# Statistics pieces summed in another order and partly ahead of the LoRA passage, and a weight chunk clipped ahead of a low half

## The chip, the cores and the metric

The kernel runs on one core of a Trainium2 chip. The metric is the device time of one execution in microseconds, median of the runs. TensorE is called PE, VectorE DVE, ScalarE ACT, GpSimd POOL; SP is the sync engine, which here only issues DMAs ("SPq" in rows; "ACTq" is ACT's own issuing).

## The reference

The input is 32 sequences of 64 tokens of width 1024, 2048 tokens in all. Cut to what matters:

```
y   = einsum('bct,bcd->bdt', x, W_cond[cond_id])          # 64x64 per sequence
h   = relu(layernorm(y @ gw1.T + gb1)); gates = h @ gw2.T + gb2; top-2 of 8, softmax, capacity
x1  = x + y @ weight.T + lora(y, gates)                   # LoRA of rank 16 for each of 8 experts
z   = x1 @ W1[adapter_id[b]].T                            # one of 8 full 1024x1024 matrices per sequence
# bitlinear(x, w): s = mean|w|; q = round(clip(w/(s+eps), -1, 1)); x @ (q*s).T
out = x1 + bitlinear(bitlinear(z, w_gate) * bitlinear(z, w_up), w_down)       # inner width 2752
```

So the mean of |w| over each of w_gate, w_up and w_down (2.8 million values each) must be known before the first weight of that layer is quantized.

## The kernel before

Every engine has a hand-written program; their order against each other comes from semaphores alone. The text splits each float32 operand into a float16 high part (ACT) and a low part (DVE). The stages:

**Main loop** (to about 245 us). `main(t)` multiplies token tile t (128 tokens, 16 tiles) by the first weight. Around it run the gate network (`quarter_mean`, `quarter_prod`, `quarter_top` on DVE), `w_step` (splits the adapter matrices and stores them to `w1s_scratch`), and `sum_gate(p)`, ACT's 16 sums of |w_gate|, placed by the table `SUMS_AT`; SP's `load_sum` fetches them.

**Passage** (about 235 to 261 us). PE transposes the weighted LoRA activations, ACT and DVE split them (`tmpw_high`, `tmpw_low`), PE does `lora(0)`.

**Slots k = 0 to 12** (261 to 450 us), and then some more. A slot is a pair of sequences with the same adapter; `linear(k)` multiplies it by its matrix (48 matmuls, L845), `linear_t(k-1)` transposes the slot before (8 matmuls, L678). An adapter in use is a rank; `load_rank(r)` (L519, two DMA transposes of 2 MB) fills one of two buffers of `w1_t`, and is on SP's queue. Into the same slots are laid `turn_x1`, `lora` and `x1_sum` of token tiles (tables `TURNS`, `LORAS`), and 24 statistics pieces of 0.92 MB: even p are w_up and are summed by ACT (`sum_up`, L1153), odd p are w_down and are summed by DVE (`sum_down`, L1586). `PIECES_AT` says in which slot k a piece is summed. ACT and DVE do the sums of slot k first, then `x1_part`/`low_x1`, `copy_z`, `x1_sum`, `high_z`/`low_z`. The pieces lie in six buffers; a load waits for the sum that frees its buffer, on the queue that issues it. `high_z` and `low_z` read two registers by TENSOR_LOAD (L391).

**Token group 0** (about 475 to 713 us). The 22 chunks n of 128 inner rows are loaded, clipped (`quantize`, DVE L1617), rounded (`round_q`, ACT L1184; the gate rows of even chunks DVE), transposed (`turn_q`, PE L884), taken out of PSUM (`store_q`, ACT L1200), summed into seven combinations (`turn_a`, `turn_b` on DVE) and stored by SP for the later groups; `gate_up(n)` (PE L900, 32 matmuls) multiplies them by the 512 tokens of the group, `scale_gate` (ACT L1205) and `product` (DVE L1661) join them, `high_inter` (ACT) and `low_inter` (DVE L1634, 128x1792) split the result. A `store_q` of an even chunk's w_down waits for the store of `wb` of the pair before. The kinds are 0 gate, 1 up, 2 down; `turn_q(2,...)` of kind 2 shares its PSUM bank with kind 0 of chunks below 3.

**Groups 1 to 3** (780 to 1398 us) use the stored combinations (L965, L1002).

Of the kernel before, what the change touches and what calls it, by code (L numbers as in the profile page):

```python
# [110 lines left out]
def build_program(nc, x, adapter_id, cond_id, cond_w, w0, lora_a, lora_b, gw1, gb1, ln_g, ln_b, gw2, gb2,  # L111
                  w1, w_gate, w_up, w_down, out):
    ctx = ExitStack()
    with ctx:
# [148 lines left out]
        index_step = sem("index_step")  # L263
# [17 lines left out]
        gate_step = sem("gate_step")  # L281
        quarter_step = sem("quarter_step")
        var_ready = sem("var_ready")
        gap_ready = sem("gap_ready")
# [3 lines left out]
        gate_exp = sem("gate_exp")  # L288
# [12 lines left out]
        w1_loaded = sem("w1_loaded")  # L301
        piece_loaded = [sem(f"piece_loaded{i}") for i in range(NSD)]
# [111 lines left out]

        def load_piece(eng, p):
            at_p, n = piece_cols(p)
            if p >= NSD:
                eng.wait_ge((up_summed, down_summed)[p % 2], (p - NSD) // 2 + 1)
            eng.dma_start(stat_in[p % NSD][:, 0:n], (up_flat, down_flat)[p % 2][:, at_p:at_p + n])\
               .then_inc(piece_loaded[p % NSD], 16)  # L420

        def piece_count(p):

            return 16 * (gate_pieces(p % NSD) + p // NSD + 1)
# [22 lines left out]

        def gate_pieces(s):

            return len(range(s, NPIECE_G, NSG)) if s < NSG else 0  # L450
# [9 lines left out]
        def _(sp):  # L460
# [16 lines left out]
            def load_sum(p):  # L477
                s = p % NSG
                if p < NSG:
                    sp.wait_ge(ag_high, 3)  # L480
                    sp.wait_ge(ag_low, 3)
                wait_if(sp, gate_summed, p - NSG + 1)
                sp.dma_start(stat_gate[s], gate_flat[:, p * PIECE_G:(p + 1) * PIECE_G]).then_inc(piece_loaded[s], 16)
# [190 lines left out]
        def _(pe):  # L674
# [333 lines left out]

            turn_q(2, 0, 1, (2,))
            gate_up(1, 1)  # L1010
# [21 lines left out]
        def _(act):  # L1032
# [34 lines left out]
            def sum_gate(p):  # L1067
                s = p % NSG
                act.wait_ge(piece_loaded[s], 16 * (p // NSG + 1))
                act.activation(stat_gate[s], stat_gate[s], ACT.Abs, accum_out=stat_g[:, p:p + 1]).then_inc(gate_summed, 1)  # L1070
# [25 lines left out]
            for m in range(1, NT + 1):  # L1096
# [9 lines left out]
                if m == NT - 3:  # L1106
                    gate_root(3)
                    act.wait_ge(gap_ready, 1)
                    act.activation(row[:, 5, :], row[:, 4, :], ACT.Exp).then_inc(gate_exp, 1)
# [8 lines left out]
                for p in SUMS_AT.get(m, ()):  # L1118
                    sum_gate(p)
            for i in range(2):  # L1120
                act.wait_ge(tmpw_transposed, i + 1)
                high(tmpw_t[:, 0, i * D:(i + 1) * D], pair[i][:, :], 1.0).then_inc(tmpw_high, 1)
# [27 lines left out]
            def sum_up(p):  # L1150
                at_p, n = piece_cols(p)
                act.wait_ge(piece_loaded[p % NSD], piece_count(p))
                act.activation(stat_in[p % NSD][:, 0:n], stat_in[p % NSD][:, 0:n], ACT.Abs,  # L1153
                               accum_out=stat_u[:, p // 2:p // 2 + 1]).then_inc(up_summed, 1)

            for k in range(LAST_TURN + 1):
# [97 lines left out]
            scale_gate(0, 0)  # L1254
            high_z(k - 1)
# [46 lines left out]
        def _(v):  # L1302
# [9 lines left out]
            def then(instruction):  # L1312
                step[0] += 1
                instruction.then_inc(index_step, 1)
                v.wait_ge(index_step, step[0])
# [25 lines left out]
            v.tensor_scalar(ix_lt, nums, ix_part, None, ALU.is_gt).then_inc(index_step, 1)  # L1341
            v.tensor_scalar(ix_le, nums, ix_part, None, ALU.is_ge).then_inc(index_step, 1)
            v.tensor_scalar(ix_shift, nums, 1.0, ix_part, ALU.add, ALU.is_equal).then_inc(index_step, 1)
# [63 lines left out]
            count = [0]  # L1407

            def gthen(instruction):
                count[0] += 1  # L1410
                instruction.then_inc(gate_step, 1)
                v.wait_ge(gate_step, count[0])
# [66 lines left out]
            def gate_weights():  # L1479
                v.tensor_tensor(gap, p2, p1, ALU.subtract).then_inc(gap_ready, 1)  # L1480
# [3 lines left out]
                v.wait_ge(gate_exp, 1)  # L1484
# [71 lines left out]
            with v.If(used > NADP - 1):  # L1556
                w_step(NT - 2)
                w_step(NT - 1)
            for i in range(2):
# [22 lines left out]

            def sum_down(p):
                at_p, n = piece_cols(p)
                v.wait_ge(piece_loaded[p % NSD], piece_count(p))
                v.tensor_reduce(stat_d[:, p // 2:p // 2 + 1], stat_in[p % NSD][:, 0:n], X, ALU.add,  # L1586
                                apply_absolute_value=True).then_inc(down_summed, 1)
# [209 lines left out]
            turn_a(1, 1)  # L1797
            product(0, 0, 0, 0)
# [7 lines left out]
            for m in range(1, 4):  # L1806
                if m > 1:
                    product(m - 1, (m - 1) % 2, (m - 1) // 2, (m - 1) // 2 % 2)
                if m == 3:
                    low_inter(0, 0)  # L1810
                quantize(m + 2, m % 2, m // 2 + 1)
# [13 lines left out]
            for m in range(16, IC + 1):  # L1825
                product(m - 1, (m - 1) % 2, (m - 1) // 2, (m - 1) // 2 % 2)
                if m % 2 == 1:
                    low_inter((m - 3) // 2, (m - 3) // 2 % 2)
                if m < IC - 2:
                    quantize(m + 2, m % 2, m // 2 + 1, last=(m == IC - 3))  # L1830
# [38 lines left out]
```

## Time and profile before

| what | value |
|---|---|
| median of 3 runs | 1390.0 us (1388.51 to 1393.92) |
| the profiled execution's own time | 1399.73 us |
| its span | 1398.1 us |
| granted TensorE clock, mean | 0.987 |
| busy: PE / DVE / ACT / POOL | 1334.7 / 727.5 / 410.5 / 141.8 us |
| mean DMA rate | 216 GB/s |

The span is the time from the first to the last instruction of the profiled execution. PE is busy for 95% of it, so the time can only fall where PE stands still, runs at the lower clock or has less to do.

### The profile page before, as it was taken

What the parts mean: (1) busy time and instruction counts of PE and PEld (TensorE: products, weight loads), DVE (VectorE), ACT (ScalarE), POOL (GpSimd) and SP (SyncE); (2) the same over time, 40 slices, a digit from 0 to 9 for tenths busy, and PEclk for the clock granted to TensorE, in tenths of its full rate; (3) what the DMA queues carried; (4) which work ended last, traced back from release to release, by engine and by line L of the source; (5) the groups of instructions that cost most, each with busy time, mean ns of one, the idle gap of its engine ahead of it and who ended that gap; (6) DMA issues with size and microseconds to landing.
All of it is one profiled execution on the core that took longest, in us unless ns stands there. A gap on an engine that the chain in (4) does not pass through costs nothing.

```text
span 1398.1 us, 23462 instructions
## 1 busy us (share of the span) xinstructions
PE 1334.7 (95%) x8864; PEld 848.3 (61%) x8864; DVE 727.5 (52%) x1187; ACT 410.5 (29%) x456; POOL 141.8 (10%) x79
## 2 busy tenths in 40 slices
PE   6999999999799998999999999999999999999998
PEld 5566664444345544555444788844888844888833
DVE  5447656443344336888855355572455581455521
ACT  3445432232231426777730011110111110111100
POOL 3200000000000000000000132210133310232200
PEclk9999999999899999999999999999999999999999
DMA  9899983999948347999774644444633355544344
GB/s 250 285 388 352 342 307 82 308 287 242 257 170 201 87 141 249 332 333 331 251 267 162 219 158 158 147 184 161 222 139 144 141 215 180 186 158 158 136 184 143
DMA packets 171950, 302.48 MB, mean 216 GB/s; under 512 B 99009, under 2 KB 131009, under 8 KB 164065
## 3 DMA queue, kind: packets, MB, share of 16 engines
q1 hardware_dynamic: 158496, 260.00, 57.0%
q10 hardware_dynamic: 12352, 40.90, 8.1%
q8 instruction: 52, 0.85, 0.2%
q0 software_dynamic: 1024, 0.53, 0.2%
q14 instruction: 26, 0.20, 0.0%
HBM read 212.39 MB, written 68.03 MB: 201 GB/s over the span
## 4 chain that ended last, share of the span: by engine, by line
PE 71%; DMA 7%; DVE 7%; issue 5%; ACT 4%; SPq 3%; ACTq 1%; POOL 1%; POOLq 0%; DVEq 0%
PE pair L965 26%; PE pair L1002 14%; PE pair L763 11%; PE pair L845 10%; SPq L519 3%; DMA wb_scratch<-region_q 2%; DMA region_q<-wb_scratch 2%; PE pair L731 2%; PE pair L900 2%; PE pair L678 2%; ACT region_q L1184 2%; PE pair L746 2%; DVE region_q L1617 1%; DMA region_w<-in_L_ffn_w_down 1%; PE pair L781 1%
## 5 line engine op out<-in xcount | busy, mean ns | idle before, releaser
L965 PE MATMUL pair<-act_t,region_q 128*128 128x256 f16 x3696 | 404.0, 273 | 0.6 <-DMA region_q<-wa_scratch 0.6
L965 PEld LDWEIGHTS pair<-act_t,region_q 128*128 128x128 f16 x3696 | 361.6, 98 | 43.3 <-DMA region_q<-wa_scratch 1.1
L1002 PE MATMUL pair<-region_q,region_w 128*128 128x512 f16 x1232 | 269.3, 381 | 6.6 <-DMA region_q<-wb_scratch 6.3
L663 POOL TENSOR_TENSOR region_w<-region_q,region_w 128x1792 f32 (+1 forms) x33 | 118.4, 3587 | 1157.7 <-ACT region_w L1209 1157.7
L1002 PEld LDWEIGHTS pair<-region_q,region_w 128*128 128x128 f16 x1232 | 120.4, 98 | 154.2 <-DMA region_q<-wb_scratch 8.1
L845 PE MATMUL pair<-region_w,act_t 128*128 x816 | 186.7, 386 | 3.7 <-issue 2.1
L763 PE MATMUL pair<-region_w,act_t 128*128 128x512 f16 x768 | 169.5, 380 | 0.0
L900 PE MATMUL pair<-act_t,region_q 128*128 128x512 f16 x704 | 157.6, 383 | 0.0
L845 PEld LDWEIGHTS pair<-region_w,act_t 128*128 x816 | 81.0, 99 | 98.1 <-issue 11.6
L1215 ACT ACTIVATE region_q<-pair 128x512 f32<-128x512 f32 x33 | 19.7, 598 | 403.3 <-PE pair L965 403.3
L1306 DVE SCALAR_TENSOR_TENSOR act_t<-pair,act_t 128x512 f32 (+1 forms) x66 | 61.1, 947 | 146.2 <-ACT act_t L1034 146.2
L763 PEld LDWEIGHTS pair<-region_w,act_t 128*128 128x128 f16 x768 | 75.1, 98 | 87.6 <-issue 1.3
L900 PEld LDWEIGHTS pair<-act_t,region_q 128*128 128x128 f16 x704 | 68.6, 99 | 79.8 <-issue 3.0
L1034 ACT ACTIVATE act_t<-pair 128x512 f32 (+1 forms) x66 | 51.3, 804 | 155.5 <-PE pair L731 54.7
L1209 ACT ACTIVATE region_w<-region_q 128x1792 f32 (+1 forms) x44 | 74.6, 1695 | 65.2 <-DVE region_q L1654 65.2
L1728 DVE SCALAR_TENSOR_TENSOR region_q<-pair,out_c,region_q 128x512 f32<-128x512 f32 x32 | 24.0, 750 | 112.1 <-PE pair L1002 112.0
L1200 ACT ACTIVATE region_q<-pair 128x1024 f16<-128x1024 int16 x66 | 63.2, 1034 | 27.1 <-DMA wb_scratch<-region_q 26.1
L1681 DVE TENSOR_TENSOR region_q<-pair,region_q 128x512 f32<-128x512 f32 x33 | 22.8, 692 | 90.1 <-PE pair L965 90.1
L678 PE MATMUL pair<-ident,region_q 128*128 128x128 f32 x328 | 48.0, 297 | 20.1 <-DVE act_t L1306 17.0
L1184 ACT ACTIVATE region_q<-region_q,inv 128x1024 f32<-128x1024 f32 x55 | 59.8, 1150 | 19.9 <-DVE region_q L1617 19.9
L1674 DVE TENSOR_TENSOR region_q<-pair,region_q 128x512 f32<-128x512 f32 x33 | 22.8, 692 | 75.6 <-PE pair L965 75.6
L678 PEld LDWEIGHTS pair<-ident,region_q 128*128 128x128 f32 x328 | 41.5, 153 | 29.1 <-issue 14.5
(187 smaller groups left out, 1024.9 us busy)
## 6 DMA issues: line engine op xcount, KB each, us to landing
region_q<-wa_scratch SPq DMA_DIRECT2D x33, 1792.0 KB, 7.4
region_q<-wb_scratch SPq DMA_DIRECT2D x28, 1408.0 KB, 6.1
region_q<-in_L_cond_weight SPq DMA_DIRECT2D x40, 512.0 KB, 8.6
w1s_scratch<-region_q ACTq DMA_DIRECT2D x40, 512.0 KB, 6.1
wa_scratch<-region_q SPq DMA_DIRECT2D x22, 896.0 KB, 5.9
region_w<-in_L_ffn_w_gate SPq DMA_DIRECT2D x16, 688.0 KB, 9.2
wb_scratch<-region_q SPq DMA_DIRECT2D x11, 896.0 KB, 4.1
region_q<-in_L_ffn_w_gate SPq DMA_DIRECT2D x19, 512.0 KB, 5.2
```

Source lines behind the costliest of these rows:

```text
L663: pool.tensor_tensor(at(iop[:, 1], u), st[s][:, 0:7], at(iop[:, 0], u), ALU.subtract)\
L678: mm = pe.transpose(dst[:, k * P:(k + 1) * P], src[:, k * P:(k + 1) * P], idn[:, :])
L763: mm = pe.matmul(acc[:, h * H:(h + 1) * H], act_t[:, a, k, t * P:(t + 1) * P], w0_t[:, 4 * h:4 * h + 4, b, k, :], start=(k == 0 and a + b ...
L845: mm = pe.matmul(pair[s][:, h * H:(h + 1) * H], act_t[:, a, c, ds(at, P)], w1_t[:, ds(buf, 1), b, c, h * H:(h + 1) * H].rearrange("p x o - ...
L900: mm = pe.matmul(dst, wa[s][:, first + k // 4, (k % 4) * P:(k % 4 + 1) * P], act_t[:, a, k, 0:GRP], start=(k == 0 and a == 0), stop=(k == ...
L965: mm = pe.matmul(bank(s_bank, b)[:, (1 - h) * HALF:(2 - h) * HALF], ring_a[s][:, h, o_a, k], moving[a], start=(opens and h == 1 and k == 0 ...
L1002: mm = pe.matmul(bank(s_bank, b), iop[:, a, p, o_a, tp * P:(tp + 1) * P], ring_b[r][:, p], start=(opens and p == 0 and a == 0), stop=(not ...
L1034: return act.activation(dst, src, ACT.Copy, scale=scale)
L1184: act.activation(tile, tile, ACT.Copy, bias=ROUND, scale=inv[:, kind:kind + 1])\
L1200: act.activation(dst, src, ACT.Copy, bias=-BITS).then_inc(q_out[kind], 1)
L1209: act.activation(at(iop[:, 0], u), st[s][:, 0:7], ACT.Copy).then_inc(inter_high, 1)
L1306: return v.scalar_tensor_tensor(out=dst, in0=src, scalar=scale, in1=hi, op0=ALU.mult, op1=ALU.subtract)
```

## The change

The semaphores `index_step` and `gate_step` become one, `gap_ready` joins `var_ready` and `gate_exp` joins `gate_std`; w_gate's sums get semaphores of their own (`gate_loaded`). The last six sums of |w_gate| move up. Pieces 0 to 3 are loaded ahead of `load_rank(0)` and summed ahead of the passage's splits; the slots' table of pieces changes; at the start of group 0 `gate_up(1)` comes ahead of the down rows of chunk 2, and chunk 3 is clipped earlier; in the loop of group 0 `quantize` comes ahead of `low_inter`.

```
-SUMS_AT = {**{m: (m - 1,) for m in range(1, 11)}, 11: (10, 11), 12: (12, 13), 13: (14, 15)}
+SUMS_AT = {**{m: (m - 1,) for m in range(1, 11)}, 11: (10, 11, 12), 12: (13, 14, 15)}
-PIECES_AT = {0: range(0, 4), 1: range(4, 6), 2: range(6, 8), 3: range(8, 12), 5: range(12, 18), 9: range(18, 24)}
-LATE_PIECES_AT = 6
+PIECES_AT = {0: range(4, 8), 1: range(8, 10), 3: range(10, 16), 6: range(16, 22), 9: range(22, 24)}
...
+        def piece_slot(p):
+            return p if p < 4 else (p - 4) % NSD
         def load_piece(eng, p):
...
-            if p >= NSD:
-                eng.wait_ge((up_summed, down_summed)[p % 2], (p - NSD) // 2 + 1)
+            if 4 <= p < 8 or p >= 10:
+                eng.wait_ge((up_summed, down_summed)[p % 2], (p - (4 if p < 8 else NSD)) // 2 + 1)
...
 # SP
-            sp.wait_ge(y_done, NT)
-            sp.wait_ge(quarter_step, 3 * (QT + 1))
-            sp.wait_ge(gate_summed, NPIECE_G)
             for s in range(4):
                 sp.wait_ge(w_stored[s], stores(0))
-            load_rank(0)
...
             for p in range(4):
                 load_piece(sp, p)
+            sp.wait_ge(y_done, NT)
+            sp.wait_ge(quarter_step, 3 * (QT + 1))
+            sp.wait_ge(gate_summed, NPIECE_G)
+            load_rank(0)
+            for p in range(4, 8):
+                load_piece(sp, p)
             sp.wait_ge(tmpw_transposed, 2)
-            for p in range(4, 6):
+            for p in range(8, 10):
                 load_piece(sp, p)
...
                 if r == 1:
-                    for p in range(6, 12):
+                    for p in range(10, 16):
                         load_piece(sp, p)
                 if r == 2:
-                    for p in range(12, 18):
+                    for p in range(16, 22):
                         load_piece(sp, p)
 # PE
-            turn_q(2, 0, 1, (2,))
             gate_up(1, 1)
+            turn_q(2, 0, 1, (2,))
 # ACT
+            for p in (0, 2):
+                sum_up(p)
             for i in range(2):
                 act.wait_ge(tmpw_transposed, i + 1)
...
-                if k == LATE_PIECES_AT:
-                    for p in range(18, NPIECE):
+                if k == 6:
+                    for p in range(22, NPIECE):
                         load_piece(act, p)
...
             scale_gate(0, 0)
+            store_q(2, 0, 1, (0, 1))
             high_z(k - 1)
...
-                store_q(m + 1, (m + 1) % 2, (m + 1) // 2, (0, 1, 2) if m == 1 else (2, 0, 1))
+                if m == 2:
+                    store_q(2, 0, 1, (2,))
+                if m > 1:
+                    store_q(m + 1, (m + 1) % 2, (m + 1) // 2)
 # DVE
+            for p in (1, 3):
+                sum_down(p)
             for i in range(2):
                 v.wait_ge(tmpw_high, i + 1)
...
             turn_a(1, 1)
+            quantize(3, 1, 1)
             product(0, 0, 0, 0)
...
                     product(m - 1, (c - 1) % 2, 2 * i + (c - 1) // 2, (c - 1) // 2 % 2)
+                    quantize(m + 2, c % 2, 2 * i + c // 2 + 1)
                     if c % 2 == 1:
                         low_inter(2 * i + (c - 3) // 2, (c - 3) // 2 % 2)
-                    quantize(m + 2, c % 2, 2 * i + c // 2 + 1)
```

The same swap of `quantize` and `low_inter` stands in the rounds ahead of and behind the loop.

On SP's queue, between the end of the main loop's loads and the wait for `main_done` that precedes `load_rank(1)`, before (the piece loads are L419, the rank's transposes L519, and rank 0's two stand ahead of these rows):

```order
L419 DMA region_q<-in_L_ffn_w_up 128x1835
L419 DMA region_q<-in_L_ffn_w_down 128x1835
L419 DMA region_q<-in_L_ffn_w_up 128x1835
L419 DMA region_q<-in_L_ffn_w_down 128x1835
L419 DMA region_w<-in_L_ffn_w_up 128x1835 [waits tmpw_transposed]
L419 DMA region_w<-in_L_ffn_w_down 128x1835
L541 COMPARE_AND_BRANCH [waits main_done]
L519 DMA_TRANSPOSE region_w<-w1s_scratch 128x8x1024 [waits w1_loaded]
L519 DMA_TRANSPOSE region_w<-w1s_scratch 128x8x1024
```

And the same place of the changed kernel, up to the same point (L421 and L516 are its lines for these):

```order
L421 DMA region_q<-in_L_ffn_w_up 128x1835
L421 DMA region_q<-in_L_ffn_w_down 128x1835
L421 DMA region_q<-in_L_ffn_w_up 128x1835
L421 DMA region_q<-in_L_ffn_w_down 128x1835
L516 DMA_TRANSPOSE region_w<-w1s_scratch 128x8x1024 [waits gate_summed,quarter_step,y_done]
L516 DMA_TRANSPOSE region_w<-w1s_scratch 128x8x1024
L421 DMA region_q<-in_L_ffn_w_up 128x1835 [waits up_summed]
L421 DMA region_q<-in_L_ffn_w_down 128x1835 [waits down_summed]
L421 DMA region_q<-in_L_ffn_w_up 128x1835 [waits up_summed]
L421 DMA region_q<-in_L_ffn_w_down 128x1835 [waits down_summed]
L421 DMA region_w<-in_L_ffn_w_up 128x1835 [waits tmpw_transposed]
L421 DMA region_w<-in_L_ffn_w_down 128x1835
```

Four pieces have moved ahead of rank 0's transposes, and four more, which wait for the sums of the first four, stand between rank 0's and rank 1's.

On PE, behind the last transposition of a slot and up to the loop of group 0, before (L884 is `turn_q`, L900 `gate_up`):

```order
L928 UNCONDITIONAL_BRANCH
L884 MATMUL pair<-ident,region_q 128x128 [waits q_out0,rounded2]
L884 MATMUL pair<-ident,region_q 128x128 x7
L900 MATMUL pair<-act_t,region_q 128x512 [waits gate_scaled,q_out1,q_out0]
L900 MATMUL pair<-act_t,region_q 128x512 x31
L1012 UNCONDITIONAL_BRANCH [waits slots_done]
```

After:

```order
L927 UNCONDITIONAL_BRANCH
L899 MATMUL pair<-act_t,region_q 128x512 [waits gate_scaled,q_out1,q_out0]
L899 MATMUL pair<-act_t,region_q 128x512 x31
L883 MATMUL pair<-ident,region_q 128x128 [waits q_out0,rounded2]
L883 MATMUL pair<-ident,region_q 128x128 x7
L1011 UNCONDITIONAL_BRANCH [waits slots_done]
```

The 32 matmuls of `gate_up(1)` no longer stand behind the transposes that wait for ACT's `store_q` of chunk 2.

On DVE, in the body of the loop of group 0, from the product of an even chunk on, before:

```order
L1661 TENSOR_TENSOR region_q<-pair,region_q 128x2x256 [waits inter_low,gate_scaled]
L1634 ISA [waits inter_high]
L1634 TENSOR_TENSOR region_w<-region_q,region_w 128x1792
L1617 TENSOR_SCALAR region_q<-region_q,clip,nclip 128x1024 [waits wq_loaded1]
L1617 TENSOR_SCALAR region_q<-region_q,clip,nclip 128x1024 [waits wq_loaded3]
L1617 TENSOR_SCALAR region_q<-region_q,clip,nclip 128x1024 [waits wq_loaded5]
L1640 TENSOR_TENSOR region_q<-region_q 128x512 [waits q_out1,q_out0]
```

After:

```order
L1667 TENSOR_TENSOR region_q<-pair,region_q 128x2x256 [waits inter_low,gate_scaled]
L1623 TENSOR_SCALAR region_q<-region_q,clip,nclip 128x1024 [waits wq_loaded1]
L1623 TENSOR_SCALAR region_q<-region_q,clip,nclip 128x1024 [waits wq_loaded3]
L1623 TENSOR_SCALAR region_q<-region_q,clip,nclip 128x1024 [waits wq_loaded5]
L1640 ISA [waits inter_high]
L1640 TENSOR_TENSOR region_w<-region_q,region_w 128x1792
L1646 TENSOR_TENSOR region_q<-region_q 128x512 [waits q_out1,q_out0]
```

The low half (L1634, then L1640) now stands behind the three clips of the odd chunk, and still ahead of `turn_a`.

## Rows read from the trace of the kernel before

**Rows 1.** The page's chain that ended last, by engine

```profile
PE 71%; DMA 7%; DVE 7%; issue 5%; ACT 4%; SPq 3%; ACTq 1%; POOL 1%; POOLq 0%; DVEq 0%
```

**Rows 2.** PE's waits from 225 to 720 us: total us, times, longest

```profile
PE pair L678 <- DVE act_t L1306: 17.0, 5, 11.7
PE pair L884 <- ACT region_q L1184: 9.4, 18, 2.0
PE pair L884 <- ACT region_q L1200: 5.5, 2, 5.1
```

**Rows 3.** The chain in order of time around slot k = 5: start, us, what

```profile
341.53 14.86 DMA region_w<-in_L_ffn_w_down
...
359.86 1.94 PE pair L678 x8
361.80 7.05 PE pair L845 x24
...
369.72 5.18 PE pair L845 x24
```

**Rows 4.** One stretch by windows: busy us by engine, PEclk, DMA share, GB/s

```profile
353.00:358.00 5.00, 0.00 (x0) 0.00 (x0) 2.52 (x2) 3.22 (x4) 0.00 (x0) 0.50 1.14 321
```

**Rows 5.** SP's queue over time: the transposes of ranks 0, 1 and 2

```profile
235.45 16.09 SPq L519 DMA_TRANSPOSE region_w<-w1s_scratch  x2
...
257.36 30.76 SPq L519 DMA_TRANSPOSE region_w<-w1s_scratch  x2
...
299.01 39.95 SPq L519 DMA_TRANSPOSE region_w<-w1s_scratch  x2
```

**Rows 6.** The timeline between slots 2 and 3: idle before and its releaser in brackets

```profile
298.59 2.06 DVE L1586 TENSOR_REDUCE stat_d<-region_q 128x1 f32<-128x1835 f32 x1 [5.99 <-DMA region_q<-in_L_ffn_w_down]
...
302.04 1.07 PE L678 MATMUL pair<-ident,region_q 128*128 128x128 f32 x8 [1.81 <-DVE act_t L1306]
...
303.86 7.01 PE L845 MATMUL pair<-region_w,act_t 128*128 x24 [0.76 <-issue]
```

**Rows 7.** The timeline in slot 8, PE

```profile
398.22 1.09 PE L678 MATMUL pair<-ident,region_q 128*128 128x128 f32 x8 [2.38 <-DVE act_t L1306]
...
399.15 5.74 PE L845 MATMUL pair<-region_w,act_t 128*128 x18
```

**Rows 8.** Register loads on ACT from 389 to 397 us: ns min/median/max

```profile
L391 ACTq TENSOR_LOAD <-ixi x2: 1072/1130/1187, 392.7 to 394.1; - x2
```

**Rows 9.** Groups of the piece sums (of both, 4 more in region_w)

```profile
L1586 DVE TENSOR_REDUCE stat_d<-region_q 128x1 f32<-128x1835 f32 x8 | 16.4, 2060 | 18.9 <-DMA region_q<-in_L_ffn_w_down 18.9
...
L1153 ACT ACTIVATE region_q<-region_q 128x1835 f32<-128x1835 f32 x8 | 13.9, 1736 | 17.3 <-DMA region_q<-in_L_ffn_w_up 14.5 <-DVE region_q L1510 2.8
```

**Rows 10.** The timeline before and in the passage, ACT and DVE

```profile
215.35 0.14 DVE L1477 COPY region_w<-region_w 1x1 f32<-1x1 f32 x1
...
244.75 1.94 ACT L1034 ACTIVATE region_q<-pair 128x1024 f16<-128x1024 f32 x2 [9.44 <-PE pair L814]
...
254.69 1.22 DVE L1510 SCALAR_TENSOR_TENSOR region_q<-pair,act_t 128x1024 f32<-128x1024 f32 x1 [6.53 <-PE pair L781]
```

**Rows 11.** The timeline at the start of group 0, PE

```profile
514.13 7.07 PE L900 MATMUL pair<-act_t,region_q 128*128 128x512 f16 x32
...
527.20 1.01 PE L884 MATMUL pair<-ident,region_q 128*128 128x128 f16 x8 [5.12 <-ACT region_q L1200]
...
528.00 9.32 PE L900 MATMUL pair<-act_t,region_q 128*128 128x512 f16 x32
```

**Rows 12.** One pair of chunks in the loop of group 0, DVE and ACT

```profile
600.24 2.02 DVE L1634 TENSOR_TENSOR region_w<-region_q,region_w 128x1792 f32 x1
...
602.44 2.86 ACT L1200 ACTIVATE region_q<-pair 128x1024 f16<-128x1024 int16 x3 [2.89 <-DMA wb_scratch<-region_q]
```

**Rows 13.** The last chunk of group 0, ACT's rounding

```profile
694.96 1.15 ACT L1184 ACTIVATE region_q<-region_q,inv 128x1024 f32<-128x1024 f32 x1 [1.13 <-DVE region_q L1617]
...
696.35 2.19 ACT L1184 ACTIVATE region_q<-region_q,inv 128x1024 f32<-128x1024 f32 x2 [0.24 <-DVE region_q L1617]
```

More of the change, by code:

```diff
@@ L262, in build_program @@
         consts_ready = sem("consts_ready")
-        index_step = sem("index_step")
+        scalar_step = sem("scalar_step")
         index_sorted = sem("index_sorted")
@@ L301, in build_program @@
         w1_loaded = sem("w1_loaded")
+        gate_loaded = [sem(f"gate_loaded{i}") for i in range(NSG)]
         piece_loaded = [sem(f"piece_loaded{i}") for i in range(NSD)]
@@ L413, in piece_cols @@
             return p // 2 * PIECE, min(PIECE, INNER * D // P - p // 2 * PIECE)
+        def piece_slot(p):
+            return p if p < 4 else (p - 4) % NSD
         def load_piece(eng, p):
             at_p, n = piece_cols(p)
-            if p >= NSD:
-                eng.wait_ge((up_summed, down_summed)[p % 2], (p - NSD) // 2 + 1)
-            eng.dma_start(stat_in[p % NSD][:, 0:n], (up_flat, down_flat)[p % 2][:, at_p:at_p + n])\
-               .then_inc(piece_loaded[p % NSD], 16)
+            s = piece_slot(p)
+            if 4 <= p < 8 or p >= 10:
+                eng.wait_ge((up_summed, down_summed)[p % 2], (p - (4 if p < 8 else NSD)) // 2 + 1)
+            eng.dma_start(stat_in[s][:, 0:n], (up_flat, down_flat)[p % 2][:, at_p:at_p + n]).then_inc(piece_loaded[s], 16)
         def piece_count(p):
-            return 16 * (gate_pieces(p % NSD) + p // NSD + 1)
+            s = piece_slot(p)
+            return 16 * len([o for o in range(p + 1) if piece_slot(o) == s])
         def store_wa(eng, p, h, n):
@@ L446, in stores @@
             return 32 * (r + 1)
-        def gate_pieces(s):
-            return len(range(s, NPIECE_G, NSG)) if s < NSG else 0
         def x1_stores(i):
@@ L1007, in down @@
                                 mm.then_inc(dn_done if tp == 0 else step_done, 1)
+            gate_up(1, 1)
             turn_q(2, 0, 1, (2,))
-            gate_up(1, 1)
             pe.wait_ge(slots_done, 1)
@@ L1068, in sum_gate @@
                 s = p % NSG
-                act.wait_ge(piece_loaded[s], 16 * (p // NSG + 1))
+                act.wait_ge(gate_loaded[s], 16 * (p // NSG + 1))
                 act.activation(stat_gate[s], stat_gate[s], ACT.Abs, accum_out=stat_g[:, p:p + 1]).then_inc(gate_summed, 1)
@@ L1107, in _ @@
                     gate_root(3)
-                    act.wait_ge(gap_ready, 1)
-                    act.activation(row[:, 5, :], row[:, 4, :], ACT.Exp).then_inc(gate_exp, 1)
+                    act.wait_ge(var_ready, 5)
+                    act.activation(row[:, 5, :], row[:, 4, :], ACT.Exp).then_inc(gate_std, 1)
                 j = m - 1
@@ L1119, in _, with sum_up @@
                     sum_gate(p)
+            def sum_up(p):
+                at_p, n = piece_cols(p)
+                act.wait_ge(piece_loaded[piece_slot(p)], piece_count(p))
+                act.activation(stat_in[piece_slot(p)][:, 0:n], stat_in[piece_slot(p)][:, 0:n], ACT.Abs,
+                               accum_out=stat_u[:, p // 2:p // 2 + 1]).then_inc(up_summed, 1)
+            for p in (0, 2):
+                sum_up(p)
             for i in range(2):
@@ L1147, in high_z @@
                 high(act_t[:, 0, :, ds(d1, SEQ)], ps8[2][:, :, SEQ:P], ACT_SCALE).then_inc(z_high, 1)
[L1150 to L1154, printed above, removed]
             for k in range(LAST_TURN + 1):
@@ L1313, in then @@
                 step[0] += 1
-                instruction.then_inc(index_step, 1)
-                v.wait_ge(index_step, step[0])
+                instruction.then_inc(scalar_step, 1)
+                v.wait_ge(scalar_step, step[0])
             def compare(dst, row, column, op, scale=None):
@@ L1404, in main_part @@
                                        in1=rows_of(x_nat[slot]), op0=ALU.mult, op1=ALU.add).then_inc(acc_released, 1)
-            count = [0]
             def gthen(instruction):
-                count[0] += 1
-                instruction.then_inc(gate_step, 1)
-                v.wait_ge(gate_step, count[0])
+                step[0] += 1
+                instruction.then_inc(scalar_step, 1)
+                v.wait_ge(scalar_step, step[0])
             def per_channel(a, n=NT):
@@ L1558, in _, with sum_down @@
                 w_step(NT - 1)
+            def sum_down(p):
+                at_p, n = piece_cols(p)
+                v.wait_ge(piece_loaded[piece_slot(p)], piece_count(p))
+                v.tensor_reduce(stat_d[:, p // 2:p // 2 + 1], stat_in[piece_slot(p)][:, 0:n], X, ALU.add,
+                                apply_absolute_value=True).then_inc(down_summed, 1)
+            for p in (1, 3):
+                sum_down(p)
             for i in range(2):
@@ L1808, in _ @@
                     product(m - 1, (m - 1) % 2, (m - 1) // 2, (m - 1) // 2 % 2)
+                if m > 1:
+                    quantize(m + 2, m % 2, m // 2 + 1)
                 if m == 3:
                     low_inter(0, 0)
-                quantize(m + 2, m % 2, m // 2 + 1)
                 if m % 2 == 0:
@@ L1826, in _ @@
                 product(m - 1, (m - 1) % 2, (m - 1) // 2, (m - 1) // 2 % 2)
+                if m < IC - 2:
+                    quantize(m + 2, m % 2, m // 2 + 1, last=(m == IC - 3))
                 if m % 2 == 1:
                     low_inter((m - 3) // 2, (m - 3) // 2 % 2)
-                if m < IC - 2:
-                    quantize(m + 2, m % 2, m // 2 + 1, last=(m == IC - 3))
                 if m < IC and m % 2 == 0:
```

20 lines of the change are left out of this document (6 added, 14 removed).

## The prediction, as put on record before the changed kernel ran

> **What bounds the kernel now.** First the page's chain by engine: PE holds 71% of it, every other engine 7% or less [rows 1]. PE is busy for 95% of the span, so the time falls only where PE stands or runs at the lower clock; DVE and ACT have slack nearly everywhere, and the groups behind 780 us read nothing that the change touches. Then PE's waits from 225 to 720 us: 17.0 us in five waits of the slots' transposition (L678) for DVE's `copy_z` (L1306), one of them 11.7; 5.5 in two waits of `turn_q` (L884) for ACT's `store_q`, one of them 5.1; 9.4 in 18 waits of `turn_q` for ACT's rounding, none above 2.0 [rows 2]. The first two are places that the change touches. The chain around slot 5 shows what is late in the worst one: a transfer of a w_down piece of 14.86 us ends it at 341.53 + 14.86 = 356.4, and PE starts its transposition only at 359.86 [rows 3]. In the window 353 to 358 PE does nothing at all, DVE and ACT do sums, and the granted clock is 0.50 [rows 4], the lower level of 1.2 GHz; the first 24 matmuls behind it take 7.05 us, the next 24 take 5.18 [rows 3].
>
> Why so late: on SP's queue pieces 12 to 17 stand behind rank 2's transposes, which start at 299.01 and take 39.95 us [rows 5], so they are issued from 339.0 and are summed in slot 5, ahead of `copy_z`.
>
> **The stall of slot 5.** The change sums these pieces (p = 16 to 21 in its numbers) in slot 6 and issues them behind a rank 2 that has less beside it. What it removes: 11.7 of waiting [rows 2], 1.94 - 1.07 = 0.9 of slow transposition [rows 3, 6], 7.05 - 5.18 = 1.9 of slow matmuls [rows 3]: **14.5 us**, if the pieces are there in time.
>
> Are they? The two transposes of a rank move the same bytes each time and took 16.09 us for rank 0, 30.76 for rank 1, 39.95 for rank 2 [rows 5]. Rank 0 ran with no piece issued ahead of it, rank 1 and 2 with pieces of the same queue still in flight. In the change four pieces go ahead of rank 0; rank 0 itself waits for the last step of `quarter_top(2)`, whose last copy is at 215.35 [rows 10], so it starts at about 215.5, 20 us earlier than now. Pieces 4 to 9 follow at 231 to 251 as the sums in the passage free their buffers. Rank 1 still waits for `main_done` (257.36 [rows 5]); I take 16 to 22 us for it, since only the tail of pieces 8 and 9 is beside it, so it ends near 274 to 280 instead of 288. Pieces 10 to 15 are then issued some 10 us earlier than 6 to 11 are now, and land at about 291 (six pieces of 0.92 MB at the 321 GB/s of [rows 4] are 17 us). Rank 2 waits for slot 2 (299.01) as before, finds them landed, and ends at about 317; pieces 16 to 21 land by about 335, and slot 6 wants them at about 347. That is 12 us of slack; with a rank 2 as slow as the present 39.95, they would land near 356 and be 9 us late.
>
> Here a page of the Trainium skill speaks against such a reordering: "DMA: Bandwidth & Descriptors", section "Issuing engines are not separate DMA queues", says that transfers of all issuing engines interleave on the same 16 DMA engines, so order alone buys no bandwidth. The trace agrees in so far as the same transposes differ by 16.09 against 39.95 with pieces beside them. By that rule the wait only moves, which is the first rival below; the order still decides who is late.
>
> **Slots 2 and 3.** Between them PE waits 1.81 for `copy_z`, another 0.76 in front of the matmuls, and then runs 24 matmuls in 7.01 instead of 5.18, because DVE idled 5.99 us for a piece [rows 6]: 1.81 + 0.76 + 1.83 = 4.4. In the change slot 3 holds three sums on DVE instead of two (2.06 each, so 6.2 us [rows 9]), all landed 7 us ahead of it. Such a chain of three sums ahead of `copy_z` can leave a wait of its own; I put 0.3 to it. **4.1 us.**
>
> **Slot 8.** PE waits 2.38 and then does 18 matmuls in 5.74 [rows 7] where 18/24 of 5.18 are 3.9. In the same slot ACT's register loads take 1.1 us each [rows 8]; pieces 18 to 23 are in flight there (issued from ACT's queue in slot 6), and in the change only 22 and 23 are. The other waits of this kind without a cause share 17.0 - 11.7 - 2.38 - 1.81 = 1.1 us, so some 0.6 of 2.38 may stay: 1.8 + 1.8, say **3.5 us** (bounds 0 and 4.2).
>
> **The passage.** The new sums stand ahead of the splits. ACT's two take 2 x 1.74 = 3.5 us [rows 9], and it has 9.44 us of idle time ahead of its splits (L1034 [rows 10]): hidden. DVE's two take 4.1; they stand behind its last work of the main loop and push `tmpw_low` by about 3.5 us, and DVE's idle of 6.53 in front of L1510 [rows 10] takes that up: PE's `lora(0)` (L781), which waits for the low half, would still find it there with 1.7 us to spare. **0**; if that cover is gone, each us is one us of PE, and SP's pieces 8 and 9 behind it are late by as much. The upper bound is 4.1 lost. The sums of |w_gate| that move up lie in ACT's idle time of the main loop and only free rank 0 earlier.
>
> **Start of group 0.** Now the transposition of chunk 2's down rows waits 5.12 us for ACT, takes 1.01, and `gate_up(1)` follows in 9.32 where a run of the same 32 at full clock takes 7.07 [rows 11]: 5.12 + 1.01 + 9.32 = 15.4 from the end of `linear_t` at 522.1. In the change `gate_up(1)` goes first: 7.07, then 8 transpositions (0.6 at full clock) and a wait of about 1.2 before chunk 3's, since ACT must do `scale_gate` and `store_q` of kind 2 first: 8.9. That frees PE by 6.5 and starts `scale_gate` of chunk 1, and with it DVE, 8 us earlier. PE and the DVE-ACT chain drive the loop behind it together; I take **7.0**. The clips of chunk 3 (2 x 1 to 3 us) fit into DVE's wait for that product. Bounds: 4.0 (only the clock and a part of the wait) to 8.1.
>
> **The swap in the loop.** `low_inter` (2.02 us) now comes behind the clips of the odd chunk, which come 2 us earlier. ACT ahead of the odd chunk's `store_q` waits 2.89 us for the store of `wb` to land [rows 12], not for a clip, and PE's waits for rounding are half a us each [rows 2]. The even chunk's chain (clips, transposes, `turn_b`, store, `store_q`, rounding, `scale_gate`, product) doesn't contain the odd clips. **0** (bounds -3 to +3 over 9 pairs). Only in the last chunk, where there is no further pair, does ACT wait for clips, 1.13 and 0.24 [rows 13]; they come 2 us earlier: **1.4**.
>
> **Sum.** 14.5 + 4.1 + 3.5 + 7.0 + 1.4 = 30.5, less 0.5 for new small waits: 30. The profiled execution took 1399.7 (span 1398.1), which is 9.7 above the median; 1399.7 - 30 = 1369.7 for one like it, and from the median 1390.0 - 30 = **1360**.
>
> **Rivals.**
> *The wait moves.* Rank 1 or 2 stays near 31 to 40 us, because pieces 8, 9 or 10 to 15 are still in flight beside it, and one of slots 3 and 6 stalls as slot 5 does now. For it: two of three ranks do so now [rows 5]. Against it: the times above leave rank 2 alone. It gives back 14.5: 1374.5.
> *No gain at the start of group 0.* ACT's `store_q` of kind 2, now behind `scale_gate`, holds `turn_q` of chunk 3 for as long as PE waits now. For it: the same `store_q` is the releaser in [rows 11]. Against it: it has the 7.07 us of `gate_up(1)` to be done in. 1367.
> *The clip was the bound of the loop.* If the 2.02 of `low_inter` was on the chain of each pair, nine pairs give 18 us more: 1342. Against it: ACT's releaser is a DMA [rows 12].
> *Slower than before.* Six pieces are now issued behind each of ranks 1 and 2. If slots 3 and 6 both find their last piece late, each loses as slot 5 does now, s, and the time is 1360 + 2s. With s = 14.5 it is 1389, no change; from s = 18.5 on, the last piece landing 4 us later relative to its sum than now, the kernel is slower by over 0.5%.
>
> **Chances.** The forecast 0.60, the wait that moves 0.15, no gain at group 0 0.12, the loop 0.03, slower 0.04, several of the terms short together (1376 to 1390) 0.06. The range 1352 to 1376 goes down by the bounds of group 0, slot 8 and the loop and up to the two likelier rivals. 0.5%, about what a measurement here can tell, is 7 us; faster by more 0.88, within it 0.07, slower 0.05.
>
> **What would show it.** In the profile after: rank 1 and rank 2 at 16 to 25 us each; no wait of the slots' transposition above 1.5 us and no 24 matmuls in 7 us; no idle time of DVE for a piece in slots 3 and 6; ACT's and DVE's new sums ahead of the splits with no new wait of PE in the passage; `gate_up(1)` at 7.07 directly behind the slots' last transposition, then a wait of about 1.2; ACT in the loop still released by the store of `wb`; no wait for a clip in the last chunk. Wrong it would be with a rank at 30 to 40 us and a piece landing behind the sum that wants it, with a wait of PE for the low half of the passage, or if the loop's pairs change their length by more than 0.3 us.

## The result and the profile after

The changed kernel takes 1377.3 us (median of 4 runs, 1376.5 to 1379.1) against 1389.3 for the one before; the ratio is 0.991 with a 95% interval of 0.989 to 0.993. It is faster, by 12 us and not by the 30 that were forecast, and 1377.3 lies just outside the range. The profiled execution took 1379.1 us (span 1377.5), the one of before 1399.7 (span 1398.1): between these two the difference is 20.6.

PE's waits in the changed kernel, from 225 to 720 us (line, what it waited for, total us, times, longest), the answer to [rows 2]:

```profile
PE pair L883 <- ACT region_q L1185: 8.1, 16, 1.9
PE pair L899 <- issue: 5.1, 1, 5.1
PE pair L677 <- DVE act_t L1311: 2.8, 4, 1.3
PE pair L883 <- ACT region_q L1201: 1.6, 2, 1.2
...
PE pair L780 <- DVE region_q L1514: 0.6, 1, 0.6
```

Three of the forecasts show at once. The 17.0 us of waits for `copy_z` are 2.8, so the stall of slot 5 is gone and didn't come back in slot 3 or 6. The 5.5 for `store_q` are 1.6, of which the one wait of 1.2 was forecast. But a wait of 5.1 us has appeared at `gate_up` (L899, before L900), and "issue" as its releaser means that the profile sees nothing that it waited for.

SP's transposes of ranks 0, 1 and 2 in the changed kernel, the answer to [rows 5]:

```profile
215.44 17.37 SPq L516 DMA_TRANSPOSE region_w<-w1s_scratch  x2
...
257.24 21.38 SPq L516 DMA_TRANSPOSE region_w<-w1s_scratch  x2
...
298.26 18.73 SPq L516 DMA_TRANSPOSE region_w<-w1s_scratch  x2
```

They start where they were forecast and take 17 to 21 us instead of up to 40. DVE finds its pieces in slot 6 without a wait (the timeline; L1311 is `copy_z` and the low halves, L1566 a piece's sum):

```profile
349.51 1.29 DVE L1311 SCALAR_TENSOR_TENSOR act_t<-pair,act_t 128x512 f32 x2 [3.44 <-ACT act_t L1033]
350.72 4.03 DVE L1566 TENSOR_REDUCE stat_d<-region_q 128x1 f32<-128x1835 f32 x2
354.66 2.05 DVE L1566 TENSOR_REDUCE stat_d<-region_w 128x1 f32<-128x1835 f32 x1
```

The start of group 0 is where the forecast broke. PE in the changed kernel there, the answer to [rows 11]:

```profile
500.96 1.04 PE L677 MATMUL pair<-ident,region_q 128*128 128x128 f32 x8
507.12 8.72 PE L899 MATMUL pair<-act_t,region_q 128*128 128x512 f16 x32 [5.12 <-issue]
515.67 0.61 PE L883 MATMUL pair<-ident,region_q 128*128 128x128 f16 x8
517.53 1.51 PE L883 MATMUL pair<-ident,region_q 128*128 128x128 f16 x24 [1.25 <-ACT region_q L1201]
```

The order is the new one, yet PE stands for the same 5.12 us as before, to the second decimal, now ahead of `gate_up(1)`. ACT's `scale_gate` and `store_q` of this place had ended by 503.7. The window 507 to 512 shows what comes after the standstill (columns as in [rows 4]):

```profile
507.00:512.00 5.00, 4.88 (x15) 1.89 (x16) 1.51 (x4) 1.78 (x2) 0.00 (x0) 0.66 0.03 9
```

The granted clock is 0.66 there, so part of these 5 us is at the level of 1.2 GHz, and the 32 matmuls take 8.72 instead of 7.07. What PE's queue did is in the view of one line, L927, the conditional blocks of the three optional slots (durations in ns, min/median/max, then first and last start):

```profile
L927 PEldq COMPARE_BRANCH  x3: 219/402/6147, 500.1 to 506.7; - x3
```

One branch took 6.15 us, from 500.1 to 506.2. The kernel before has the same three branches, at its L928:

```profile
L928 PEldq COMPARE_BRANCH  x3: 219/405/6147, 520.1 to 526.8; - x3
```

Where the 20.6 us between the two profiled executions lie, by three milestones: the end of the slots' last transposition came at 522.1 and comes at 502.0, 20.1 earlier; from there to the first down-projection matmul it took 191.2 us (to 713.3) and takes 192.3 (to 694.3), 1.1 longer; the rest took 684.8 and takes 683.2. All of the gain is in the slots (the 1.1 and the 1.6 behind them nearly cancel), and group 0, from which 8.4 were expected, gave nothing.

### The profile page after: what moved, and what is told of

It reads as the page before. It is cut to its first block, busy times and chain, and to the rows that moved or that the text cites. A ratio compares the mean times of both kernels' runs of the same rounds, so it can differ in the third digit from the quotient of the medians.

```text
span 1377.5 us, 23462 instructions
## 1 busy us (share of the span) xinstructions
PE 1326.7 (96%) x8864; PEld 843.8 (61%) x8864; DVE 727.0 (53%) x1187; ACT 409.9 (30%) x456; POOL 141.8 (10%) x79
## 4 chain that ended last, share of the span: by engine, by line
PE 73%; DVE 7%; DMA 6%; issue 5%; ACT 4%; SPq 2%; ACTq 1%; POOL 1%; POOLq 0%; DVEq 0%
PE pair L964 27%; PE pair L1001 15%; PE pair L844 11%; PE pair L762 11%; DMA region_q<-wb_scratch 3%; DMA wb_scratch<-region_q 3%; PE pair L899 2%; PE pair L730 2%; PE pair L677 2%; PE pair L745 2%; ACT region_q L1185 1%; PE pair L780 1%; ACT region_q L1201 1%; DVE region_q L1623 1%; SPq L500 1%
## 5 line engine op out<-in xcount | busy, mean ns | idle before, releaser
L844 PE MATMUL pair<-region_w,act_t 128*128 x816 | 181.7, 379 | 3.1 <-DVE act_t L1311 1.6
L899 PE MATMUL pair<-act_t,region_q 128*128 128x512 f16 x704 | 158.6, 385 | 5.1 <-issue 5.1
L1311 DVE SCALAR_TENSOR_TENSOR act_t<-pair,act_t 128x512 f32 (+1 forms) x66 | 61.1, 946 | 142.2 <-ACT act_t L1033 142.1
L899 PEld LDWEIGHTS pair<-act_t,region_q 128*128 128x128 f16 x704 | 68.8, 99 | 86.0 <-issue 9.7
L1185 ACT ACTIVATE region_q<-region_q,inv 128x1024 f32<-128x1024 f32 x55 | 59.6, 1149 | 17.7 <-DVE region_q L1623 17.3
L1311 DVE SCALAR_TENSOR_TENSOR region_q<-region_q 128x1024 f16<-128x1024 f32 x40 | 47.4, 1219 | 7.2 <-ACT region_q L1033 7.1
```

Source lines behind the costliest of these rows:

```text
L844: mm = pe.matmul(pair[s][:, h * H:(h + 1) * H], act_t[:, a, c, ds(at, P)], w1_t[:, ds(buf, 1), b, c, h * H:(h + 1) * H].rearrange("p x o - ...
L899: mm = pe.matmul(dst, wa[s][:, first + k // 4, (k % 4) * P:(k % 4 + 1) * P], act_t[:, a, k, 0:GRP], start=(k == 0 and a == 0), stop=(k == ...
L1185: act.activation(tile, tile, ACT.Copy, bias=ROUND, scale=inv[:, kind:kind + 1])\
L1311: return v.scalar_tensor_tensor(out=dst, in0=src, scalar=scale, in1=hi, op0=ALU.mult, op1=ALU.subtract)
```

## The experiments

Each is told with its median and the ratio to the kernel before on the same chip, with the 95% interval. Across the three chips the kernel before took 1391.5 (17 runs, 1384 to 1396), 1389.7 (11) and 1389.3 us (12).

**The kernel before again.** No edit.

> The kernel before, unchanged, for a second profile. Theory A (the profiled execution of before, 1399.7, was one with an unusually long stall in the slots; the forecast subtracted a stall that most executions have only in part): time 1388 to 1394, rank 2's transposes well under 39.95 us, and PE's wait in slot 5 some 3 to 6 us instead of 11.7. Rival (the 9.7 us above the median lie outside the slots): the wait of slot 5 is 11 to 12 us again, in an execution of about 1390.

It took 1394.2 us. Its rank 2 and its PE in slot 5:

```profile
300.27 32.86 SPq L519 DMA_TRANSPOSE region_w<-w1s_scratch  x2
...
354.95 1.94 PE L678 MATMUL pair<-ident,region_q 128*128 128x128 f32 x8 [8.74 <-DVE act_t L1306]
356.89 7.40 PE L845 MATMUL pair<-region_w,act_t 128*128 x24
```

The wait of slot 5 is 8.7 and not 11.7, rank 2 takes 32.9 instead of 40.0, and behind slot 2 PE waits 0.35 for `copy_z` and runs at full clock, where [rows 6] have 1.81 and 7.01 (the 0.76 in front of the matmuls is there again). The wait lies above the 3 to 6 us expected and below the rival's 11 to 12, in an execution that was itself a long one. A third profile, that of the next kernel, has the slots of before and took 1388.9 us (span 1387.3), close to the median. Its rank 2 took 30.90, and its slot 5:

```profile
351.78 1.94 PE L678 MATMUL pair<-ident,region_q 128*128 128x128 f32 x8 [7.26 <-DVE act_t L1310]
353.72 6.49 PE L845 MATMUL pair<-region_w,act_t 128*128 x24
```

So in the three profiles the stall is the longer the longer rank 2's transposes take (30.9, 32.9, 40.0 us with 7.3, 8.7, 11.7 of wait), these vary from one execution to the next, and the first profile had drawn long ones. The slots of this third profile end at 513.4, 8.7 us ahead of those of the first and 11.4 behind those of the changed kernel (502.0).

**Only the edits of group 0.** The kernel before with

```diff
-            turn_q(2, 0, 1, (2,))
             gate_up(1, 1)
+            turn_q(2, 0, 1, (2,))
```

and the matching edits of ACT and DVE, the swap of the clips in the loop included.

> The kernel before with only the edits of token group 0 (gate_up(1) first, chunk 3 clipped earlier, clips ahead of low_inter). Theory A (PE's wait there is its queue's branch over the optional slots, not ACT's copy): no gain, 1388 to 1391, PE idle for about 5.1 us ahead of gate_up(1), whose 32 matmuls take 8.5 to 9.3 us. Rival B: 1382, no such idle time.

1390.4 us, ratio 1.000 (0.998 to 1.002). PE:

```profile
518.58 9.40 PE L900 MATMUL pair<-act_t,region_q 128*128 128x512 f16 x32 [5.17 <-issue]
```

The group-0 edits alone are worth nothing, with the same standstill and the same slow matmuls.

**Only the pieces and the passage.** The changed kernel with group 0 as before.

> The changed kernel with its edits of token group 0 undone (start of group 0 and loop as before); new order of pieces and passage. Theory A: all of the gain is here, 1377 us (ratio 0.990 to 0.993). Rival B (the start of group 0 gains what was forecast and the pieces gain less): 1383 to 1386.

1376.1 us, ratio 0.990 (0.987 to 0.992): the whole gain, and not less than the full change's.

**One number.** The kernel before with

```diff
-... 3: range(8, 12), 5: range(12, 18), 9: range(18, 24)}
+... 3: range(8, 12), 6: range(12, 18), 9: range(18, 24)}
```

and every load where it was.

> The kernel before with one number changed: pieces 12 to 17 are summed in slot 6 instead of slot 5, every load where it was. If the later sum does the work: the last piece lands 350 to 356 us into the span, slot 6 wants it at about 350, so PE waits 2 to 6 us there instead of 7 to 12 and the time is 1383 to 1386, half of the gain. Rival (the earlier loads behind an undisturbed rank 2 are needed for any of it): the stall moves to slot 6 whole, 1389 to 1391.

1378.4 us, ratio 0.993 (0.991 to 0.996), more than expected. Its rank 2 still took 32.46 us, its last piece was issued at 336.11, and yet DVE waited for no piece:

```profile
350.25 1.29 DVE L1306 SCALAR_TENSOR_TENSOR act_t<-pair,act_t 128x512 f32 x2 [2.83 <-ACT act_t L1034]
351.46 4.03 DVE L1586 TENSOR_REDUCE stat_d<-region_q 128x1 f32<-128x1835 f32 x2
355.40 2.05 DVE L1586 TENSOR_REDUCE stat_d<-region_w 128x1 f32<-128x1835 f32 x1
```

The pieces had landed when slot 6 came to them. This profile is of the shortest of the seven runs; they spread from 1376.0 to 1388.3, the changed kernel's four from 1376.5 to 1379.1. A slow rank 2 would explain the long ones, as it does before, but none of them was profiled. The later sum brings most of the gain; what the earlier rank 0 and shorter rank 2 add seems to be evenness rather than time.

**PE without the optional slots.** The changed kernel with

```diff
-            pairs = field(pe, F_CUM, NADP - 1, NSLOT)
-            for n in range(k, NSLOT):
-                with pe.If(pairs > n):
-                    if n == k:
-                        pe.wait_ge(prod_done, 1)
-                    linear(n, n % 2)
-                    linear_t(n, n % 2)
```

taken out of PE's program alone. It leaves out the multiplication of slots 13 and up, which this input doesn't have, and the register load ahead of the branches.

> The changed kernel, in which PE's program leaves out the three optional slots and their branches (with this input they are skipped, so the output is the same). Theory A: the idle time of 5.12 us ahead of gate_up(1) goes, its 32 matmuls take 7.07 instead of 8.72, chunk 3's transposition follows after a wait near the forecast 1.2; 6 to 7 us less, 1370 to 1372. Rival B (PE waits there for work of ACT or DVE): 1377, the wait stays.

1367.1 us, ratio 0.982 (0.979 to 0.985), 10 us less than the changed kernel and more than expected:

```profile
500.68 1.04 PE L677 MATMUL pair<-ident,region_q 128*128 128x128 f32 x8
501.72 7.07 PE L899 MATMUL pair<-act_t,region_q 128*128 128x512 f16 x32
508.62 0.61 PE L883 MATMUL pair<-ident,region_q 128*128 128x128 f16 x8
510.48 1.52 PE L883 MATMUL pair<-ident,region_q 128*128 128x128 f16 x24 [1.25 <-ACT region_q L1194]
```

This is the sequence that was forecast, row by row: no standstill, 7.07, 0.61, a wait of 1.25. Beyond the 5.1 + 1.65 of the standstill and the clock, it lacks another loss of the changed kernel, which is told below (1.4 + 1.6 us).

**The group-0 edits priced without the branch.** Both kernels lack PE's optional slots and ran on one chip. The first has group 0 as before:

> pieces_only (token group 0 in the order of before) with PE's optional slots left out. Theory A2 (ACT's copy of chunk 2 and the branch end within 0.5 us of each other, so either hides the other): turn_q of chunk 2 still waits 4.5 to 5.1 us for ACT, gate_up(1) stays slow, 1374 to 1376, so that the edits of group 0 are worth 7 to 9 us once the branch is gone. Rival (only the branch costs): the wait goes, 1366 to 1368.

1375.4 us, ratio 0.990 (0.988 to 0.992).

```profile
506.72 1.01 PE L883 MATMUL pair<-ident,region_q 128*128 128x128 f16 x8 [4.85 <-ACT region_q L1194]
507.53 8.68 PE L899 MATMUL pair<-act_t,region_q 128*128 128x512 f16 x32
```

With the branch gone, `turn_q` waits 4.85 us for ACT after all. The second has the new start, and the loop's clips in their old place:

> after_no_optional with the swap undone (low_inter ahead of the clips again), the edits at the start of group 0 kept. As forecast for the swap: 1.4 us more than with it, all in the last chunk (a wait of PE of 2.0 for ACT's rounding there, pairs of 17.7 us unchanged), so 1368 to 1369. Rival (the swap costs something at the first pair): no difference or faster.

1369.8 us, ratio 0.986 (0.984 to 0.988). So the new start of group 0 is worth 1375.4 - 1369.8 = 5.6 us when no branch stands there (7.0 had been forecast). The traces say the same: from the end of `linear_t` to chunk 2's `gate_up` it takes 15.5 us (501.9 to 517.4) in the first and 10.1 (502.4 to 512.5) in the second. Its last chunk has the waits of before:

```profile
671.29 0.62 PE L883 MATMUL pair<-ident,region_q 128*128 128x128 f16 x8 [1.97 <-ACT region_q L1178]
```

With the swap (after_no_optional) this wait is 0.36, 1.6 us less; the pairs are 17.7 us in both. More can hang on it: behind the wait of 1.97 the last 16 transpositions and 64 matmuls take 1.89 + 14.83 us here and 1.07 + 13.98 with the swap, 1.7 less, with a granted clock of 0.66 (window 672 to 677) against 1.00 (670 to 675). These 1.7 us stand in four of the six profiles that have the wait of 1.96 to 1.98, not in that of the kernel before and not in slot6_only. The medians differ by 2.7 (1369.8 against 1367.1) on different chips, with intervals of the ratios that overlap, so the traces carry the price of the swap here and not the times.

**Fetching the branch's target early.** The changed kernel with the three optional slots in one block, jumped over by one branch, and a prefetch hint ahead of `gate_up(0)`; nothing is left out.

```diff
+            at_hint = pe.mark_branch_hint_location()
             pe.wait_ge(z_low, GRP // SEQ)
             gate_up(0, 0)
...
+            pe.br_cmp(pairs, k, comp_op="IS_LE", on_true="optional_end", on_false="optional_body").branch_hint(at_hint)
```

> The changed kernel with PE's three optional slots inside one block that a single compare-and-branch skips, and a branch prefetch hint for it ahead of the last transpositions before gate_up(0) (general, nothing left out). Theory A (the 6.15 us are the fetch of the branch's target): the branch takes well under 1 us, the idle time ahead of gate_up(1) is under 1 us, the time as in after_no_optional, 1366 to 1370. Rival C (the branch waits for PE's queue to empty or for the register, whatever is fetched): the idle time stays at 4 to 5 us, 1375 to 1378.

1371.3 us, ratio 0.987 (0.985 to 0.989), 1.3 above the range that was expected; unlike after_no_optional it still has the first pair's loss, told below. The branch and the start of `gate_up(1)`:

```profile
L927 PEldq COMPARE_BRANCH  x1: 510/510/510, 500.8 to 500.8; - x1
```

```profile
501.65 1.04 PE L677 MATMUL pair<-ident,region_q 128*128 128x128 f32 x8
502.68 7.07 PE L899 MATMUL pair<-act_t,region_q 128*128 128x512 f16 x32
```

And the same block without the hint:

> after_hint without the hint: one block round the three optional slots, skipped by one branch. If the hint (the early fetch of the target) made the difference: the branch takes 5 to 6 us again, idle 5 us ahead of gate_up(1), 1376 to 1378. Rival (one branch instead of three was it): 1370 to 1372.

1377.4 us, ratio 0.991 (0.989 to 0.993). Its branch:

```profile
L926 PEldq COMPARE_BRANCH  x1: 6654/6654/6654, 499.5 to 499.5; - x1
```

The same branch on the same place takes 0.51 us with the hint and 6.65 without, and the register load ahead of it is in both. The DMA queue that brings instructions shows what the hint moves. In the kernel without it one transfer starts between 503 and 504 us, while the branch is held (499.5 to 506.2); in the kernel with it one starts between 496 and 497, 4 us ahead of the branch (queue and kind, packets, MB, share; windows 503:504 and 496:497):

```profile
q8 instruction: 1, 0.02, 5.5%
```

```profile
q8 instruction: 1, 0.02, 6.4%
```

All eight profiles with a long branch have such a transfer inside it, about 4 us behind its start (the changed kernel at 504 to 505), and hint_and_order has it at 496 to 497, ahead of its branch of 0.51 at 501.0. So what the branch waits for is its target's code. The two kernels differ by 6.1 us, from one chip to another.

**ACT's copies in another order.** The changed kernel, in which ACT copies gate and up of an even chunk first and down last:

```diff
-                    store_q(m + 1, (c + 1) % 2, 2 * i + (c + 1) // 2)
+                    store_q(m + 1, (c + 1) % 2, 2 * i + (c + 1) // 2, (2, 0, 1) if c % 2 == 0 else (0, 1, 2))
```

> The changed kernel with ACT's store_q of even chunks in the order gate, up, down instead of down, gate, up, so that ACT copies gate and up while the store of wb lands. If the store of wb is what sets the pairs' 17.7 us: PE's waits for rounding (0.5 + 0.34 each pair) go, pairs of about 16.8 us, 7 to 8 us less, 1369 to 1371. Rival (it only moves ACT's idle time): pairs of 17.7, 1377.

1367.1 us, ratio 0.985 (0.982 to 0.987), 10 us less than the changed kernel where 7 to 8 were expected. ACT's waits for the store of `wb` from 480 to 720 us, in the changed kernel and in this one:

```profile
ACT region_q L1201 <- DMA wb_scratch<-region_q: 25.8, 9, 4.3
```

```profile
ACT region_q L1201 <- DMA wb_scratch<-region_q: 8.6, 9, 2.1
```

PE's waits for ACT's rounding fall from 8.1 to 0.8 us, and a pair takes 16.5 us instead of 17.7, which is twice the 8.25 from one `gate_up` to the next: PE has no wait left in it. So the store of `wb` did set the loop's pace through ACT, and it could be had by order alone.

**Both together.**

> after_hint and after_order together: no idle time of 5 us ahead of gate_up(1) (6 us less than the changed kernel) and pairs of 16.5 us in the loop of group 0 (10 us less): if the two add up 1361 to 1363; if the start's gain is caught up by the store of wb at the first pair, 1364 to 1367.

1359.5 us (1357.7 to 1361.2), ratio 0.978 (0.975 to 0.980): the two add up, and go 30 us below the kernel before.

## Why the prediction was wrong

**The stall of slot 5 (14.5) and what stands beside it.** The mechanism was right: with the later sum and the earlier load the wait of 11.7 is gone, rank 1 and 2 take 21.4 and 18.7 where 16 to 22 and some 18 (from 299 to 317) were put, and the waits in slots 2 and 3 and in slot 8 have shrunk (slot 8 keeps 1.26 us of 2.38; new ones of 0.61 and 0.48 stand elsewhere). Net 20.1 us between the profiled executions against 22.1 - 0.5 forecast. (The terms for slots 2 and 3 and for slot 8 set 7.01 and 5.74 of one view against 5.18 of another, in which the same 24 matmuls are 0.16 shorter; it matters little.) Which edit does it was put too much on the transposes: the one number of the slot's table brings most of it while rank 2 stays at 32 us.

**The sum against the median.** "from the median 1390.0 - 30" is the first step that failed. The 22 us were read in an execution that took 9.7 us more than the median, and they were taken off the median whole. The two further executions of these slots had 8.7 and 7.3 us of wait in slot 5, and 1.1 and 0.5 in all between slots 2 and 3: most of the 9.7 was the stalls themselves, above their usual length. In the profile near the median (group0_only) the three terms come to about 9.3 instead of 14.5 (7.26 of wait, 0.9 of slow transposition, 1.15 of slow matmuls), 0.5 instead of 4.1, and 2.8 instead of 3.5 (1.07 of wait, 0.3 and 1.45 of slow work); less the new small waits this comes close to the 11.4 us by which its slots end later. The gain in a usual run is 12 to 15 us (the full change 12.0, only the pieces 15.4 on another chip). The sentence that said how far the profiled time stands above the median should have made the slots' terms a range: at the most 22, and 22 - 9.7 = 12 if the whole excess lies in what is removed.

**The start of group 0 (7.0).** This is the second step that failed, "5.12 + 1.01 + 9.32 = 15.4", taken as a wait for ACT that the new order removes. In place of the forecast 8.9 the changed kernel takes 15.5 us from the end of `linear_t` to chunk 3's transposition (502.0 to 517.5), where the kernel before took 15.1 (522.1 to 537.2), so the gain was nothing and lay outside the bounds of 4.0 to 8.1 too. The profile named ACT's `store_q` because it ended last among what it can see; PE's own branches (520.1 to about 527.0) ended within 0.5 us of it (526.8). Each hid the other: taking away the wait for ACT (the change) gains nothing, taking away the branch alone (pieces_no_optional) leaves a wait of 4.85, and taking away both gives the forecast rows and 5.6 us. The rival "no gain at the start of group 0" was right in its result and wrong in its cause, since `store_q` didn't hold `turn_q` for longer than the forecast 1.2.
A rule of the Trainium skill would have pointed there, "Runtime: NRT & Kernel Launch", section "Instruction fetch mechanics": a taken branch whose target is not among the blocks already fetched makes the engine wait for a DMA that brings it. The runs agree, with 6.15 and 6.65 us without a hint and 0.51 with one, and with the instruction transfer inside the long branches.

**The loop and the last chunk (0 and 1.4).** The swap left the pairs at 17.7 us, as forecast, and the last chunk's wait fell by 1.6. But the changed kernel gave as much back at the first pair: ACT waited 4.32 us there for the store of `wb` where 2.8 to 2.9 is usual, PE waited 1.85 for the rounding behind it, and `gate_up` took 8.65. The store was issued at 523.97, with a chunk's three loads issued 3 to 5 us ahead of it and the store of `wa` 1.6 behind it, and landed after 6.9 us instead of 4.1. Chance alone is a poor account of it. Of the profiles with the swap, group0_only (4.55), nest_no_hint (4.22) and after_hint (4.03) show it as well, and after_order and hint_and_order have 2.08 and 2.05 there against 0.8 to 0.9 in the next pairs; after_no_optional alone doesn't (2.90). None of the six profiles with the clips in their old place has more than 2.96. So the rival put down for no_optional_no_swap, that the swap costs something at the first pair, fits six of seven profiles, though not the two kernels that were compared for it, which both lack PE's branch. By what path the swap slows this store stays open; in after_order it costs PE nothing, since ACT has other copies to do.

**The passage (0).** Right: DVE's low half ends 3 us later (251.2), `lora(0)` starts at 253.08 (253.19 before), and PE has no wait more.

**The rival that the wait moves** didn't come true in any run, and neither did the slower one. The prediction had drawn it from the DMA engines being shared whatever engine issues; that says nothing of order within SP's queue, and here order alone brought the gain: in every profile with the new order rank 1 takes 21 to 24 us and rank 2 about 19, and slot6_only gains without moving any load.

## What to carry to other kernels

When the profiled execution stands above the median, the stalls in it are candidates for the excess: take a second profile, or price a removed stall as a range down by the whole excess. A releaser named in a profile is the last that it can see; before counting on the end of such a wait, look at the waiting engine's own queue in the same stretch, above all at branches, and ask what ends second. Where a write-back's landing sets a loop's pace, first give the waiting engine its other work of the same round.

## What the runs showed of the hardware

The first compare-and-branch over an optional slot on TensorE's queue took 6.15 us, the two right behind it 0.4 and 0.2; one branch over all three slots took 6.65, and 0.51 with a hint ahead of the 32 matmuls before it. In each of the eight profiles with a long branch (6.15 to 6.65 us) one transfer of the instruction queue started inside it; with the hint it started 4 us ahead of the branch. The branches of the same blocks on ACT and DVE took 0.05 and 0.06 us. After PE had stood still for 4.9 to 5.2 us, the next 32 matmuls took 8.1 to 9.7 us instead of 7.07, part of them at the lower of the two clock levels (granted clock 0.66 in the window above). After a wait of 2.0 us and one of 0.4 the matmuls behind took 1.7 us more in four of six profiles. The two DMA transposes of a rank took 16.1 us with no piece issued ahead of them, 17 to 19 with four pieces issued 5 to 9 us ahead (rank 0 after) or six issued 14 to 20 us ahead (rank 2 after), 21 to 24 with five issued 7 to 10 us ahead (rank 1 after), and 30 to 40 with six issued in the 12 us ahead (ranks 1 and 2 before).
